# Masking the row ids on VectorE instead of GpSimd, and constant products on TensorE in the opening of a graph transformer layer

## The reference

```python
x = x + gnn(layernorm(x), adj, ...)          # x: (8, 1024, 128)
x = x + ffn(layernorm(x), ...)
# gnn: q, k, v = three projections, 4 heads of 32; scores clipped to +-10, set to -10 where adj is 0,
#      softmax within each chunk of 128 keys, times v, summed over the 8 chunks;
#      times Wo.T + bo, plus the layer's input, layernorm with gamma and beta
# ffn: the 2 best of 8 experts for each token; sum over them of gelu(t @ W1 + b1) @ W2 + b2
```

## Time and profile before

| | us |
|---|---|
| median of three runs | 759.71 (757.60 to 760.57) |
| the profiled execution, own time | 758.38 |
| its span, first to last instruction | 756.7 |
| busy: PE, DVE, ACT, POOL | 689.9, 599.9, 502.8, 583.8 |
| mean granted clock of TensorE | 0.976 |

### The profile page before, as it was taken

The page is one execution under the profiler, slowest core; times in us unless marked ns, Lnnn a source line. Parts: engine busy times, 40 slices in busy tenths (PEclk is TensorE's granted clock), DMA queues, the critical chain, the costliest instruction groups (busy, mean ns, idle before and its releaser), DMA issues.

```text
span 756.7 us, 17027 instructions
## 1 busy us (share of the span) xinstructions
PE 689.9 (91%) x5408; PEld 357.1 (47%) x5408; DVE 599.9 (79%) x1301; ACT 502.8 (66%) x1017; POOL 583.8 (77%) x685
## 2 busy tenths in 40 slices
PE   5888999999999999999999999998899999999930
PEld 2322233333333333333333333232798999999830
DVE  3788989999999999999999999998977555554410
ACT  4755577786777877777777776665865666666610
POOL 7649596988989889898898988989777755555553
PEclk9998999999999999999999999999999999999975
DMA  7630010011010111101110001051513523233300
GB/s 269 184 107 29 0 30 15 15 43 43 29 45 15 43 43 30 43 15 43 43 29 29 20 26 43 15 141 37 142 52 109 144 79 90 75 91 89 94 13 0
DMA packets 47958, 45.42 MB, mean 60 GB/s; under 512 B 6981, under 2 KB 42576, under 8 KB 47872
## 3 DMA queue, kind: packets, MB, share of 16 engines
q1 hardware_dynamic: 41888, 31.60, 14.7%
q0 software_dynamic: 5984, 12.74, 4.8%
HBM read 27.73 MB, written 18.34 MB: 61 GB/s over the span
## 4 chain that ended last, share of the span: by engine, by line
PE 67%; DVE 14%; issue 8%; ACT 5%; POOL 3%; DVEq 1%; SPq 0%; DMA 0%; POOLq 0%; ACTq 0%
PE scores_ps L453 16%; PE ctx_ps L465 11%; PE z_ps L472 9%; PE scores_ps L622 9%; DVE e L978 9%; PE ctx_ps L648 4%; PE z_ps L648 4%; ACT x_rows L764 3%; PE job_ps L492 2%; PE job_ps L501 2%; PE job_ps L528 2%; PE job_ps L557 2%; POOL out L1477 1%; PE job_ps L513 1%; PE job_ps L484 1%
## 5 line engine op out<-in xcount | busy, mean ns | idle before, releaser
L759 ACT ACTIVATE e<-e 128x2048 f32<-128x2048 f32 x128 | 245.1, 1914 | 145.0 <-DVE e L978 145.0
L978 DVE SCALAR_TENSOR_TENSOR e<-scores_ps,bound_mem 128x2048 f32<-128x2048 f32 x128 | 293.2, 2291 | 33.5 <-PE scores_ps L453 28.6
L1477 POOL DMA_INDIRECT out<-e,near x91 | 92.7, 1018 | 67.7 <-POOL near L1470 32.5
L857 ACT ACTIVATE e<-scores_ps,bound_mem 128x128 f32<-128x128 f32 x364 | 104.0, 372 | 53.0 <-PE scores_ps L622 52.4
L1450 POOL TENSOR_TENSOR ctx_part<-ctx_part,z_inv 128x1024 f32<-128x1024 f32 x60 | 115.8, 1930 | 23.8 <-DVE z_inv L994 23.8
L472 PE MATMUL z_ps<-e,one_column 128*32 128x512 f32 x1024 | 133.4, 592 | 0.0
L1462 POOL TENSOR_TENSOR ctx_sum<-ctx_sum,ctx_part 128x512 f32<-128x512 f32 x90 | 115.4, 1282 | 7.8
L622 PE MATMUL scores_ps<-e,bound_mem 128*128 128x128 f32 x728 | 97.5, 277 | 4.9 <-DVE bound_mem L1174 3.3
L622 PEld LDWEIGHTS scores_ps<-e,bound_mem 128*128 128x128 f32 x728 | 88.5, 192 | 7.8 <-issue 4.4
L986 DVE STREAM_TRANSPOSE ctx_part<-ctx_ps 128x512 f32<-128x512 f32 x128 | 90.3, 705 | 1.8 <-PE ctx_ps L465 1.8
L1424 POOL DMA_INDIRECT sorted_rows<-x_rows,slot x64 | 64.4, 1006 | 18.1 <-issue 16.9
(11 more groups left out here) (182 smaller groups left out, 1001.2 us busy)
## 6 DMA issues: line engine op xcount, KB each, us to landing
near<-sorted_rows SPq DMA_DIRECT2D x91, 130.0 KB, 2.2
near<-in_x SPq DMA_DIRECT2D x16, 256.0 KB, 2.9
bound_mem<-in_adjT SPq DMA_DIRECT2D x4, 1024.0 KB, 9.1
x_post<-in_x SPq DMA_DIRECT2D x16, 256.0 KB, 2.8
sorted_rows<-pad_row SPq DMA_DIRECT2D x1, 3640.0 KB, 15.8
out<-e,near POOLq DMA_INDIRECT x91, 2.7
sorted_rows<-x_rows,slot POOLq DMA_INDIRECT x64, 2.6
bound_mem<-in_w SPq DMA_DIRECT2D x1, 1024.0 KB, 5.6
```

Of the source, the lines that this page charges most:

```text
L759: nc.scalar.activation(every, every, ACT.Exp, scale=SCORE_SCALE).then_inc(exp_done, 1)
L857: nc.scalar.activation(e_flat[:, h_at:h_at + P], scores_ps[:, i % 2, k * P:(k + 1) * P], ACT.Gelu, bias=part_flat[:, bias_at:bias_at + 1]) ...
L978: dve.scalar_tensor_tensor(out=e[:, s % E_RING], in0=scores_ps[:], scalar=-CLIP, in1=to, op0=ALU.max, op1=ALU.min).then_inc(clipped, 1)
L1477: nc.gpsimd.indirect_dma_start(out=out_rows, out_offset=bass.IndirectOffsetOnAxis(ap=near_u[:, id_at:id_at + 1], axis=0), in_=e_flat[:, at ...
```

## The change

- `mask_id` moves from GpSimd to VectorE: in round k of the tiles it stands between `add_bias(k - 2)` and `finish(k - 2)`. GpSimd's queue has only the stores there. The instruction is an addition of unsigned 32-bit numbers, which VectorE runs in another form than GpSimd.
- TensorE gets `keep_busy(n)`: n products of a constant 128x128 tile with itself, whose result nobody reads. 16 stand at the very start, as soon as GpSimd has set the tile (`half_ready`), 3 before x block 0 is transposed, 2 behind, 2 before the first scores, 7 behind the values of block 0 and 6 behind the transposes of block 1: 36 in all.
- The two small bias products stand behind the keys and queries of block 0 instead of ahead of its transposes. ScalarE normalises x block 0 before it copies `bv` and drains the centred `wo`; the copy of x block 0 with the output bias (`add_output_bias`) comes behind the drains of keys and queries.
- x block 2 is loaded between the two halves of the adjacency matrix instead of behind both, its statistics come after the clip of step 1 instead of step 0, its square root on GpSimd after one more bound, and its normalising on ScalarE in step 2, behind the drain of block 1's keys, instead of step 1.

```diff
-            load_x(2)
...
+                if half == 0:
+                    load_x(2)
...
+            def keep_busy(n, to=scores_ps[:, 0, 0:P]):
+                for _ in range(n):
+                    pe.matmul(to, n2[:, 0, :], n2[:, 0, :], start=True, stop=True)
+
+            pe.wait_ge(half_ready, 1)
+            keep_busy(16)
             pe.wait_ge(ident_ready, 1)
             pe.wait_ge(proj_loaded, 16 * 8)
             pe.wait_ge(centre_ready, 1)
             pe.matmul(z_ps[:, 0:D], w_proj[:, W_O, :], centre[:], start=True, stop=True).then_inc(wo_filled, 1)
+            keep_busy(3)
+            turn_xn(0)
+            keep_busy(2)
+            keys(0)
+            queries(0)
             pe.wait_ge(wo_ready, 1)
             pe.wait_ge(bv_ready, 1)
             pe.matmul(z_ps[:, D:D + 1], wo_centred[:], bv_all[:], start=True, stop=False)
             pe.matmul(z_ps[:, D:D + 1], centre[:], bo_sb[:], start=False, stop=True).then_inc(bias_filled, 1)
-
-            turn_xn(0)
-            keys(0)
-            queries(0)
+            keep_busy(2)
...
                             values(0)
+                            keep_busy(7, ctx_ps[:, 0:P])
                         if j == 1:
                             turn_xn(1)
+                            keep_busy(6, ctx_ps[:, 0:P])
...
             act.wait_ge(ident_ready, 1)
+            normalise_x(0)
             nc.scalar.activation(bv_all[:], bv_sb[:], ACT.Copy, scale=float(CHUNKS)).then_inc(bv_ready, 1)
             act.wait_ge(wo_filled, 1)
             nc.scalar.activation(wo_centred[:], z_ps[:, 0:D], ACT.Copy).then_inc(wo_ready, 1)
-            normalise_x(0)
...
             drain_q(0)
+            add_output_bias(0)
             normalise_x(1)
...
                             drain_xnT(1)
-                            normalise_x(2)
                         if j == 2:
                             drain_k(1)
+                            normalise_x(2)
...
+            def mask_id(i):
+                r, of = i % XT_RING, i - MASKED_AT
+                if of == 0:
+                    dve.wait_ge(mask_ready, 1)
+                dve.wait_ge(xt_loaded[r], 16 * (i // XT_RING + 1))
+                id_u = near_u[:, xt_at[r] + ID_AT:xt_at[r] + ID_AT + 1]
+                dve.tensor_tensor(id_u, id_u, mask[:, of:of + 1], ALU.add).then_inc(id_masked, 1)
...
-                    if s == 0:
+                    if s == 1:
                         statistics_x(2)
...
                     add_bias(k - 2)
+                if MASKED_AT <= k - 2:
+                    mask_id(k - 2)
...
+            nc.gpsimd.memset(n2[:, 0, :], 0.5)
             nc.gpsimd.memset(minus_half[:], -0.5).then_inc(half_ready, 1)
...
             prepare_bound(0, HALF0_D)
+            prepare_bound(0, HALF0_D + 1)
             root(ln["1"], 2)
-            for c in range(HALF0_D + 1, CHUNKS):
+            for c in range(HALF0_D + 2, CHUNKS):
...
                 while stored < stored_by(k):
-                    if MASKED_AT <= stored:
-                        mask_id(stored)
                     store(stored)
```

More of the change, by code:

```diff
@@ L794, in drain_xnT, with add_output_bias @@
                 nc.scalar.activation(xnT[:, v % 2, :], turned_ps(v)[:], ACT.Copy).then_inc(xnT_ready, 1)
+                if v > 0:
+                    add_output_bias(v)
+            def add_output_bias(v):
                 need(act, proj_filled, done(v - 4))
                 if v == 0:
+                    act.wait_ge(bias_filled, 1)
+                    nc.scalar.activation(bo_all[:], z_ps[:, D:D + 1], ACT.Copy).then_inc(bias_ready, 1)
                     act.wait_ge(bias_ready, 1)
@@ L866, in _ @@
             nc.scalar.activation(wo_centred[:], z_ps[:, 0:D], ACT.Copy).then_inc(wo_ready, 1)
-            normalise_x(0)
-            act.wait_ge(bias_filled, 1)
-            nc.scalar.activation(bo_all[:], z_ps[:, D:D + 1], ACT.Copy).then_inc(bias_ready, 1)
             drain_xnT(0)
@@ L1462, in add_context @@
                 nc.gpsimd.tensor_tensor(to, first, ctx_part[:, at], ALU.add).then_inc(ctx_added, 1)
-            def mask_id(i):
-                r, of = i % XT_RING, i - MASKED_AT
-                if of == 0:
-                    pool.wait_ge(mask_ready, 1)
-                pool.wait_ge(xt_loaded[r], 16 * (i // XT_RING + 1))
-                id_u = near_u[:, xt_at[r] + ID_AT:xt_at[r] + ID_AT + 1]
-                nc.gpsimd.tensor_tensor(id_u, id_u, mask[:, of:of + 1], ALU.add).then_inc(id_masked, 1)
             def store(i):
```

## The result

The changed kernel takes 730.4 us, the median of four executions, against 760.14 for the kernel before on the same chip: a ratio of 0.9603, 95% interval 0.9561 to 0.9646. (One of the four took 1345.41 us, and two executions of the kernel before on another chip 974.32 and 1339.29, for reasons that no row shows; the ratios leave them out, and the median of the other three is 729.23.) A second set of five gave 729.52, ratio 0.9618 (0.9595 to 0.9642). The prediction was 730.0 in a range of 726 to 738. The profiled execution took 729.23 us, 29.15 less than the profiled one before. Its span is 726.9 us, 29.8 less: outside the span stand 2.33 us where 1.68 stood before, and no row shows why.

A forecast was written before the change was run, and what follows sets the result against it. GpSimd's late stores, slowed by its masks, were taken to bound the program's end. Gains of 25.4 us at the end and 2.8 in the opening summed to 28.2, so 758.4 became 730 us, range 726 to 738.

The forecast's parts named there:

- The end: Last tiles and stores: with masks off GpSimd, the lag and the ring's loss come back, 25.4 us together.
- the lag: GpSimd's last store, 22.45 us behind VectorE's finishing of tile 90, would follow after 0.8: 21.65 us gained.
- the ring: Late in the run SP's loads wait for stores to free places; TensorE's lost 3.76 us would come back.
- The gap behind the last `finish`: From the end of the last finishing to the last store: between 0.30 and 0.85 us, taken as 0.8.
- The mask: 70 masks on VectorE at 0.15 us each, covered by 0.38 us idle before `finish`: no cost; uncovered 10.5 us.
- the slower rival: Stores hold VectorE's masks, making VectorE the bound: at 1.15 us each, tiles take 54 us longer, 784; chance 0.02.
- the dear mask: Mask on VectorE costs 0.6 us, round 2.12 us: 15.7 us lost at the tiles, 746 us; chance 0.05.
- The opening: Before the tiles: earlier first clip 3.06 us, faster scores about 0.6, late block 2 costs 0.9; net gain 2.8 us.
- The first 16 products: Constant products at TensorE's start: would end at 7.9 us; taking over 8 us would show the forecast wrong.
- Block 2's transposes: In step 3 TensorE would wait for block 2's normalising on ScalarE, a gap of about 0.9 us.
- a rival in which it does not: Opening: clock stays low through the constant products, losing 3.4 us instead of winning 2.8: 736.4 us; chance 0.10.
- SP's waits for stores: Sign at the end of the run: SP's waits for stores, 14 from 684 us on, should vanish.

The follow-up runs named there:

- the kernel with the masks alone: The kernel before, with only the 70 masks moved to VectorE and its opening unaltered: 734.25 us, ratio 0.9677.
- the sums' experiments: The changed kernel plus unread VectorE sums beside each of 70 masks: 128 elements 730.16 us; 768 elements 730.78; 768 and 512 elements 761.29.
- the kernel with both sums: The changed kernel with two unread VectorE sums, over 768 and 512 elements, beside each of the 70 masks: 761.29 us, ratio 1.0022.
- the repeat: The changed kernel unaltered, measured a second time with one more trace of its opening: 729.52 us.
- the long sum: The changed kernel with one unread VectorE sum over 768 elements (0.94 us) beside each of the 70 masks: 730.78 us, ratio 0.9631.
- the opening alone: The changed kernel with the masks back on GpSimd: 756.32 us, ratio 0.9960.
- the three variants that had them: The changed kernel with block 2 normalised earlier and seven products in each long block 1 gap: 729.65 us; first quarter requested earlier too: 734.29; block 2 loaded earlier instead: 727.98.

## Why the prediction was right, and where it was not

**The end** (25.4 predicted) came as worked out: 21.34 for the lag and 3.87 for the ring by the trace, 25.5 by the medians of the kernel with the masks alone. The catching up at 1.29 us, the 1.9 us spacing afterwards, TensorE's even spacing at the end are all in the rows. The gap behind the last `finish` was 1.11, not 0.8: the last store waits for the store ahead of it, not for `finish`, and that one started 0.1 us after the last `finish` began.

**The total** came closer than its terms. The end was met, the opening was 1.7 us too small (4.54 against 2.8, in the traces), and 0.65 us of the shorter span were lost outside it, which the prediction had taken as 1.68. That the median is 730.4 and the forecast 730.0 is partly luck.

**The mask** (0.15 us predicted) takes 0.152. The column is minimum, median, maximum in ns:

```profile
L1208 DVE CUSTOM_DVE_ANT_0 near<-near,mask x70: 147/152/174, 586.2 to 715.8; 128x2 uint16<-128x2 uint16 x70
```

63 of the 70 lie wholly inside a store, which takes 0.98 us, and the longest took 174 ns. So no store held a mask for its length. The addition of 1.30 us, from which the slower rival took that a store might do so, began at 557.17, beside an addition on GpSimd (L1434, 1.26 us from 557.06) and beside no store. Costed at nothing, the mask cost nothing.

**The slower rival was priced wrongly**, and with it the dear mask. The step was "VectorE's round is 1.896 - 0.38 = 1.52". That takes as busy all that is not idle before `finish`. My own row showed another idle time, 25.4 us before 50 additions, named "issue", 0.51 us a tile, and a table of windows would have settled it: from 590 to 684 us VectorE of the kernel before is busy 51.17 of 94 us, 1.03 a tile (busy PE, PEld, DVE, ACT, POOL):

```profile
590.00:684.00 94.00, 94.00 (x845) 93.98 (x844) 51.17 (x197) 64.91 (x249) 56.37 (x86) 1.00 0.34 92
```

By the sums' experiments a round with the mask needs 0.87 us (less than 1.03, as each instruction there is counted only until the next one starts), of which the mask holds 0.07 (689.95 - 689.88 in the kernel with both sums). By an estimate from these, the mask would have been free up to about 1.1 us and not 0.38. At 0.6 the time would not have been 746, and at 1.15, held by the store for its whole length, some 70 x 0.05 = 3.5 us would have been lost, not 54. The forecast did not rest on this, but two of its rivals did.

**The opening** (2.8 predicted) brought more: 3.97 us by the scores of step 4 (32.83 in the trace before, 28.86 now), 3.49 in the repeat. The first 16 products take 6.08 us, less than the 8 that would have refuted the forecast, and end at 7.18 where it had 7.9; the transposes start at 8.64 (9.1 predicted). First clip 14.59 and 15.07 against the 15.05 predicted, bound by VectorE's bounds as said. The scores of step 1 gave the full 0.95 against the trace before, instead of what the constant products were to leave of it, as these stand in front of work that waits for the clip anyway. But 0.95 was read from one trace: with the masks alone the same step took 1.14 in the opening of before. Block 2's transposes wait 0.67 (0.9 predicted), 0.5 more than the 0.16 that TensorE idled there before.

By the tiles the gain is 4.54, as block 1 had one slow step fewer in this execution. That is no effect of the change that could be counted on: with the same opening, block 1 has a slow step or two in some executions (1.14 and 1.74 us for the scores at its two long waits here, 1.52 and 1.14 in the repeat, 1.98 and 1.62 with the long sum) and none in the opening alone.

**The argument for the opening was only partly right.** The forecast tied it to TensorE's level. The level does rise before block 0, and a rival in which it does not was worth 6.2 us against the forecast. Without any constant product, which is not that rival, since none stands in the way then, only 0.8 to 1.7 us were lost by the medians, and 1.8 to 2.7 by spans and scores. The rest of the opening's gain comes with the new order: bias products behind the keys, normalising ahead of the copies, and block 2's later places; no run takes these apart.

**One sign I gave was not a sign.** SP's waits for stores were to vanish. They became fewer: from 655 to 720 us SP waited 31.2 us, 26 times, before and waits 16.3 us, 13 times, now, apart from its wait for the last stores. TensorE's spacing is even all the same: SP runs up to 16 tiles ahead and waits for a place of the ring in any case. Whether the wait costs something is read from TensorE's spacing.

Left open: what sets the landing of the matrix's first quarter between 11.1 and 13.1 us, how the opening's gain divides between the constant products and the order, and which of the products are needed.

## What to carry to other kernels

An instruction whose result the next one on the same engine waits for can cost several times its own duration (here 2.08 - 1.29 = 0.79 us for a mask of 0.21); issue it one item ahead before moving it elsewhere, which did as well here (733.86 us against 734.25). The cover that an engine offers is its whole idle time in the stretch, from a window's busy sum, not the one wait in front of the instruction that interests: 0.94 us more a tile cost nothing here, where that wait was 0.38 in the kernel before. Small loads that an early wait counts should not be issued behind a large one: here `bo` landed after 6.5 us instead of 2.1, and that cost 4.8 us in the medians, together with the late load of block 1 (734.29 against 729.52). And one trace is one execution: a step that ran slow in it need not have been slow for a reason that the change removes.

## What was not expected of the hardware

- A store on GpSimd began 0.85 us after a mask on the same engine that it needed, 0.16 us after a mask when a store lay between the mask it needed and itself, 0.30 us after another store. It is not the engine that matters: with the masks on VectorE a store began 0.79 us after the end of the `finish` that it needed (716.46 against 715.38 + 0.29).
- The same idle time of 2.13 us in block 1 was followed by scores of 2.09 us in the trace before and 2.06 with the masks alone, of 1.14 in the changed kernel, and of 1.52 in its repeat. That one idle time does not decide TensorE's level. Seven constant products in the gap went with 1.14 in the three variants that had them, but so did the bare gap in the opening alone.
- The granted clock of a window reads 1.00 in the opening while products run at the lower level (2.09 us for scores that take 1.14 later); in block 1, from 60 to 65 us of the changed kernel, it reads 0.66 and agrees with the durations.
- A 1 MB load put ahead of four loads of 512 bytes made these take 5.1 to 6.5 us to land instead of 2.0 to 2.1.
